# Attention scores of 16 heads in two row strips of the TensorE array instead of one padded stack

## What is computed

```python
scores = jnp.einsum('bhid,bhjd->bhij', Q, K) / math.sqrt(DH)
scores = scores + _alibi_bias(L, scores.dtype)[None]
attn = jax.nn.softmax(scores, axis=-1)
x = jnp.einsum('bhij,bhjd->bhid', attn, V)
...
y = jax.nn.silu(xf @ wg) * (xf @ wu) @ wd        # each expert, weighted by the router
```

## Time and profile before

| | us |
|---|---|
| median of 3 runs | 236.56 |
| lowest and highest | 236.47, 237.14 |
| the profiled execution | 235.97 |
| its span, first to last instruction | 234.2 |

### The profile page before, as it was taken

How to read it: one execution, slowest core, us unless ns; L and a number is a source line. 1 busy time by engine, 2 the same in 40 slices (tenths; PEclk the granted TensorE clock), 3 DMA queues, 4 the chain that set the end, 5 groups by cost and what they waited for, 6 DMA issues and landing times.

```text
span 234.2 us, 6086 instructions
## 1 busy us (share of the span) xinstructions
PE 213.8 (91%) x1942; PEld 175.4 (75%) x1942; DVE 175.9 (75%) x612; ACT 118.3 (51%) x283; POOL 74.4 (32%) x178
## 2 busy tenths in 40 slices
PE   2969787979999999999999999999999899989995
PEld 2757455757788787977897878878897779768884
DVE  4599636995699678985899569957985788653891
ACT  8565656466426734475346443663367234763310
POOL 2500016010860159013921094107700580038000
PEclk9999999999999999999999999999999999999999
DMA  5553586223312470317032612325123600250000
GB/s 157 175 90 105 125 215 205 80 69 99 87 48 60 83 172 3 104 52 199 3 102 49 157 44 60 84 78 131 38 70 88 165 0 4 84 126 0 1 25 22
DMA packets 13079, 20.24 MB, mean 86 GB/s; under 512 B 2800, under 2 KB 9440, under 8 KB 12544
## 3 DMA queue, kind: packets, MB, share of 16 engines
q1 hardware_dynamic: 12080, 18.64, 31.2%
q10 hardware_dynamic: 976, 1.32, 1.8%
HBM read 16.03 MB, written 3.78 MB: 85 GB/s over the span
## 4 chain that ended last, share of the span: by engine, by line
issue 33%; PE 31%; DVE 17%; POOL 11%; ACT 3%; DMA 1%; DVEq 1%; ACTq 0%; POOLq 0%; SPq 0%
POOL hid L1314 6%; DVE nmax L971 6%; PE ps_up L511 5%; PE ps_pv L444 4%; PE ps_m L537 4%; PE ps_st L425 3%; PE ps_pv L451 3%; PE ps_up L516 2%; DVE tg L1075 2%; DVE stacks_sb L1202 1%; PE ps_up L308 1%; DMA ident<-in_c_ident 1%; DVE hid L1081 1%; PE ps_m L466 1%; POOL ve L1278 1%
## 5 line engine op out<-in xcount | busy, mean ns | idle before, releaser
L791 ACT ACTIVATE th<-ps_up 128x256 f32<-128x256 f32 x72 | 27.6, 383 | 35.5 <-PE ps_up L516 34.8
L735 ACT ACTIVATE probs<-ps_st 128x512 f32<-128x512 f32 x64 | 37.0, 595 | 16.3 <-PE ps_st L425 11.1
L537 PE MATMUL ps_m<-wd_sb,hid 128*128 128x128 f32 x288 | 44.8, 283 | 0.0
L971 DVE TENSOR_REDUCE nmax<-ps_s 128x4 f32<-128x512 f32 x64 | 41.9, 680 | 0.4 <-issue 0.4
L1075 DVE SCALAR_TENSOR_TENSOR tg<-th,ps_up 128x256 f32<-128x256 f32 x72 | 29.8, 414 | 13.5 <-ACT th L791 13.2
L1314 POOL TENSOR_TENSOR hid<-hid,crep 128x256 f32<-128x256 f32 x56 | 39.1, 732 | 0.2 <-issue 0.2
L537 PEld LDWEIGHTS ps_m<-wd_sb,hid 128*128 128x128 f32 x288 | 37.6, 191 | 1.0
L1081 DVE TENSOR_TENSOR hid<-tg,ps_up 128x256 f32<-128x256 f32 x72 | 29.7, 413 | 1.0
L511 PE MATMUL ps_up<-x_hi,wg_hi 128*128 128x256 f32 x72 | 26.6, 369 | 0.4 <-ACT x_hi L772 0.2
L1278 POOL TENSOR_TENSOR ve<-mv,eps_sb 128x1 f32<-128x1 f32 x16 | 3.0, 191 | 69.5 <-DVE mv L1022 69.5
L425 PE MATMUL ps_st<-stacks_sb 98*128 98x128 f16 x256 | 24.8, 220 | 0.2
(11 more groups left out here) (147 smaller groups left out, 434.2 us busy)
## 6 DMA issues: line engine op xcount, KB each, us to landing
crep<-cw_dram SPq DMA_DIRECT2D x28, 256.0 KB, 4.6
stacks_sb<-qk_dram SPq DMA_DIRECT2D x32, 128.0 KB, 3.4
qk_dram<-qk_parts SPq DMA_DIRECT2D x16, 128.0 KB, 1.8
out_y<-x_all SPq DMA_DIRECT2D x8, 128.0 KB, 4.6
wg_sb<-in_wgT ACTq DMA_DIRECT2D x1, 576.0 KB, 3.5
wu_sb<-in_wuT ACTq DMA_DIRECT2D x1, 576.0 KB, 3.3
wd_sb<-in_wd SPq DMA_DIRECT2D x1, 576.0 KB, 4.1
x_all<-in_x SPq DMA_DIRECT2D x2, 256.0 KB, 4.2
```

What stands on the lines that cost most here:

```text
L537: last = mm(ps_dn[:, b * P:(b + 1) * P], hid[:, buf, c, b * P:(b + 1) * P], wd_sb[:, c, :], start=(c == 0 and b == 0), stop=(c == SHARED), ...
L735: fn(probs[:, b, g * HG * P:(g + 1) * HG * P], scores_bank(a, g)[:], ACT.Exp).then_inc(exp_sb, 1)
L791: fn(th[:, c % 2, :], ps_up[c % 2][:, 0, :], ACT.Tanh, scale=0.5).then_inc(tanh_sb, 1)
L971: v.tensor_reduce(nmax[:, b, HG * g:HG * g + HG], ps_s[g % 2][:].rearrange("p (h j) -> p h j", h=HG), AX_X, ALU.max, negate=True).then_inc ...
```

## The change

The 16 heads are cut into two strips of 8. Strip 0 keeps its rows at partitions 0 to 33 and strip 1 at 64 to 97 (32 rows of data and two for the shift), so there are no zero rows and no memsets for them, and a tile holds 8 heads instead of 16 per partition. The products have 32 rows (`scores`) or 34 (`scores_T`) and sit in a part of the array: tiles of 32x128 and of 64x128 at row 0 and at row 64. `scores` and `scores_T` now make two groups per call, with heads of strip 0 and strip 1 in turn into two banks, and wait until both banks have been read. `ORDER` maps the position of a group to its heads (0, 2, 1, 3). Each stack DMA becomes two of half the size, and so does each `shift_rows`; the k stacks of group p now wait for the shift rows of the sequence b = 0 of group p - 1, as the q stacks did for b = 1. The orders of PE, DVE and ACT are rewritten to suit.

```diff
+STRIP = 64
 SROWS = 4 * DH
-ZROWS = 96
-AROWS = ZROWS + 2
+AROWS = SROWS + 2
+HS = H // 2
+ORDER = (0, 2, 1, 3)
...
         qk_parts = sb("qk_parts", [P, 2, 2, T], F16)
-        stacks_sb = sb("stacks_sb", [AROWS, 2, 2, H, T], F16)
+        stacks_sb = sb("stacks_sb", [STRIP + AROWS, 2, 2, HS, T], F16)
...
-        nsplit = sb("nsplit", [P, NB, 2, H], F16)
+        nsplit = sb("nsplit", [P, NB, 2, 2, HS], F16)
...
                 sp.wait_ge(s_kd, 32 * p + 32)
+                if not at_start(p):
+
+                    sp.wait_ge(s_nm[0], 32 * p)
                 for plane, row in ((2, 0), (3, 2 * DH)):
-                    src = bass.AP(qk_dram.tensor, (buf * 5 + plane) * (P * T), [[H * T, 2 * DH], [1, H * T]])
-                    sp.dma_start(stacks_sb[row:row + 2 * DH, buf, 1].rearrange("r h t -> r (h t)"), src).then_inc(s_stack, 16)
...
+                    for s in range(2):
+                        src = bass.AP(qk_dram.tensor, ((buf * 5 + plane) * P + s * HS) * T, [[H * T, 2 * DH], [1, HS * T]])
+                        at = STRIP * s + row
+                        sp.dma_start(stacks_sb[at:at + 2 * DH, buf, 1].rearrange("r h t -> r (h t)"), src).then_inc(s_stack, 16)
...
-                    sp.wait_ge(s_nm[1], 16 * p)
+                    sp.wait_ge(s_nm[1], 32 * p)
                 for row in (0, 2 * DH):
-                    src = bass.AP(qk_dram.tensor, buf * 5 * (P * T), [[H * T, 2 * DH], [1, H * T]])
-                    sp.dma_start(stacks_sb[row:row + 2 * DH, buf, 0].rearrange("r h t -> r (h t)"), src).then_inc(s_stack, 16)
+                    for s in range(2):
+                        src = bass.AP(qk_dram.tensor, (buf * 5 * P + s * HS) * T, [[H * T, 2 * DH], [1, HS * T]])
+                        at = STRIP * s + row
+                        sp.dma_start(stacks_sb[at:at + 2 * DH, buf, 0].rearrange("r h t -> r (h t)"), src).then_inc(s_stack, 16)
...
-            def scores(a, b, g, buf):
-
-
-
-                bank, n = ps_s[g % 2], 2 * NHG * a + NHG * b + g
-                if b == 0 and g == 0:
-                    pe.wait_ge(s_stack, 64 * a + 64)
+            def scores(a, b, j, buf):
+
+
+                n = 2 * NHG * a + NHG * b + 2 * j
+                if b == 0 and j == 0:
...
                 else:
-                    pe.wait_ge(max_sb, n - 1)
-                if g == 0:
-                    mm(bank[:], dist16[:], slope_hi[:, 0:HG, :], start=True, stop=False, skip_group_check=True)
-                for h in range(HG * g, HG * g + HG):
-                    o = (h - HG * g) * P
-                    last = mm(bank[:, o:o + P], qs[buf][0:ZROWS, h, b * P:(b + 1) * P],
-                              ks[buf][0:ZROWS, h, b * P:(b + 1) * P],
-                              start=(g > 0), stop=True, skip_group_check=True)
-                last.then_inc(s_mm, 1)
+                    pe.wait_ge(max_sb, n)
+                if j == 0:
+                    mm(ps_s[0][:], dist16[:], slope_hi[:, 0:HG, :], start=True, stop=False, skip_group_check=True)
+                for k in range(HG):
+                    for s in range(2):
+                        row, h = STRIP * s, HG * j + k
+                        last = mm(ps_s[s][:, k * P:(k + 1) * P], qs[buf][row:row + SROWS, h, b * P:(b + 1) * P],
+                                  ks[buf][row:row + SROWS, h, b * P:(b + 1) * P], start=(j > 0 or s > 0), stop=True,
+                                  skip_group_check=True)
+                        if k == HG - 1:
+                            last.then_inc(s_mm, 1)
...
-            def scores_T(a, b, g, buf, f=None):
-
-                bank, n = scores_bank(a, g), 2 * NHG * a + NHG * b + g
-                seeded = not at_start(a) and (b, g) in ((0, 0), (1, 0), (1, 1))
+            def scores_T(a, b, j, buf, f=None):
+
+                n = 2 * NHG * a + NHG * b + 2 * j
+                seeded = not at_start(a) and (b, j) != (0, 1)
...
                 if seeded and b == 0:
                     pe.wait_ge(seed0_sb, a)
                 elif seeded:
-                    pe.wait_ge(seed1_sb, 2 * a + g - 1)
-                elif not (at_start(a) and b == 0 and g < 2):
-                    pe.wait_ge(exp_sb, n - 1)
-                if g == 0:
-                    pe.wait_ge(s_nm[b], 16 * a + 16)
...
+                if not (at_start(a) and b == 0 and j == 0):
+                    pe.wait_ge(exp_sb, n)
+                if j == 0:
+                    pe.wait_ge(s_nm[b], 32 * a + 32)
...
-                first = False if seeded else bias(bank, g)[0]
-                for h in range(HG * g, HG * g + HG):
-                    o = (h - HG * g) * P
-                    last = mm(bank[:, o:o + P], ks[buf][:, h, b * P:(b + 1) * P], qs[buf][:, h, b * P:(b + 1) * P],
-                              start=first, stop=True, skip_group_check=True)
-                    first = False
-                last.then_inc(st_mm, 1)
...
+                first = [False if seeded else bias(scores_bank(a, 2 * j), ORDER[2 * j])[0],
+                         bias(scores_bank(a, 2 * j + 1), ORDER[2 * j + 1])[0]]
+                for k in range(HG):
+                    for s in range(2):
+                        row, h = STRIP * s, HG * j + k
+                        last = mm(scores_bank(a, 2 * j + s)[:, k * P:(k + 1) * P], ks[buf][row:row + AROWS, h, b * P:(b + 1) * P],
+                                  qs[buf][row:row + AROWS, h, b * P:(b + 1) * P], start=first[s], stop=True,
+                                  skip_group_check=True)
+                        first[s] = False
+                        if k == HG - 1:
+                            last.then_inc(st_mm, 1)
...
                 scores(a, 0, 0, abuf)
-                scores(a, 0, 1, abuf)
                 if p is not None:
                     project_q(p)
                     project_k(p)
                 late_down(0)
-                scores(a, 0, 2, abuf)
                 late_down(1)
                 expert_in_T(f)
-                scores(a, 0, 3, abuf)
+                scores(a, 0, 1, abuf)
                 late_down(2)
                 up(f, 0)
+                up(f, 1)
                 scores(a, 1, 0, abuf)
-                up(f, 1)
-                scores(a, 1, 1, abuf)
                 shift_T(a, 0)
                 router(f)
                 late_down(3)
-                scores(a, 1, 2, abuf)
                 up(f, 2)
+                scores(a, 1, 1, abuf)
                 late_down(4)
-                scores(a, 1, 3, abuf)
                 up(f, 3)
                 late_down(5)
-                scores_T(a, 0, 0, abuf)
+                scores_T(a, 0, 0, abuf, f=f)
                 late_down(6)
-                scores_T(a, 0, 1, abuf, f=f)
                 shift_T(a, 1)
                 late_down(7)
                 second_half(f, a, p, q, abuf)
             def second_half(f, a, p, q, abuf):
                 up(f, 4)
-                scores_T(a, 0, 2, abuf)
+                scores_T(a, 0, 1, abuf)
                 weights_T(f, a)
-                scores_T(a, 0, 3, abuf)
                 up(f, 5)
-                if not at_start(f): down(f - 1, (8,), abuf)
                 scores_T(a, 1, 0, abuf)
                 weigh_values(a, 0, f)
+                if not at_start(f): down(f - 1, (8,), abuf)
                 scores_T(a, 1, 1, abuf)
-                scores_T(a, 1, 2, abuf)
                 values_T(a, 0)
                 up(f, 6)
-                scores_T(a, 1, 3, abuf)
                 attention_T(a, 0, f)
                 up(f, 7)
                 weigh_values(a, 1)
...
+                g = ORDER[i]
+                act.wait_ge(st_mm, 2 * NHG * a + NHG * b + i + 1)
+                if i == 0 and not at_start(a):
                     act.wait_ge(pv_mm, 2 * a + b - 1)
-                fn(probs[:, b, g * HG * P:(g + 1) * HG * P], scores_bank(a, g)[:], ACT.Exp).then_inc(exp_sb, 1)
+                fn(probs[:, b, g * HG * P:(g + 1) * HG * P], scores_bank(a, i)[:], ACT.Exp).then_inc(exp_sb, 1)
...
             def shift_rows(a, b, buf):
                 act.wait_ge(nm_sb, 2 * a + b + 1)
-                act.dma_start(qs[buf][ZROWS:AROWS, :, b * P:(b + 1) * P], nmT[:, b, :]).then_inc(s_nm[b], 16)
+                for s in range(2):
+                    act.dma_start(qs[buf][STRIP * s + SROWS:STRIP * s + AROWS, :, b * P:(b + 1) * P],
+                                  nmT[H * s:H * (s + 1), b, :]).then_inc(s_nm[b], 16)
...
             def seed(a, g):
-                dve.wait_ge(exp_sb, 2 * NHG * a + NHG + g - 1)
-                v.tensor_copy(ps_st[(g + 1) % 2][:], bias_T[:, g, :]).then_inc(seed1_sb, 1)
+                dve.wait_ge(exp_sb, 2 * NHG * a + NHG - 1 + 2 * g)
+                v.tensor_copy(ps_st[1][:], bias_T[:, g, :]).then_inc(seed1_sb, 1)
...
-            v.memset(stacks_sb[:, 0, 0].bitcast(F32), 0.0).then_inc(dve_pads, 1)
...
-            v.memset(stacks_sb[:, 1].bitcast(F32), 0.0).then_inc(dve_pads, 1)
```

105 lines of the change are left out of this document (44 added, 61 removed).

## The result

The changed kernel takes **262.70 us** (median of 4 runs, 259.69 to 264.15) where the kernel before takes 236.51 us (235.94 to 237.14): a ratio of **1.106, interval 1.097 to 1.116**. The forecast was 252.6 us in a range of 236 to 262. Direction and main mechanism were right; the loss is 26 us where 16 were forecast, and the median lies 0.7 us above the range (as a ratio, 1.106, it is just inside: 262 to 236.56 is 1.108). The profiled execution took 264.15 us, with a span of 262.3 us. The four runs differ more than those of the kernel before, and they go with the mean granted clock of TensorE: 0.974 in the one of 259.69 us, 0.941 and 0.948 in the others.

The account below looks back on a forecast made before the run. It took PE (91% busy) as nearly the bound, but its hand-over with ACT and DVE as deciding. 235.97 + 12.3 (seven steps) + 3.7 (first group) = 252.0 us profiled, 252.6 forecast; range 236 to 262.

Parts of the forecast that it names:

- main mechanism: Steps: PE waits on ACT and DVE; six lag 1.9 us each, the last 0.9, 12.3 us in all.
- the block with three biases: Second half of a step: PE waits 1.0 us for ACT's exponential and starts 1.76 late; 0.5 wait at the next block.
- The second DMA: Second half, ACT: two half-size shift DMAs cost between nothing and 0.62 us more to issue; taken at 0.5.
- the tiles: Score blocks: products in pairs gain 1.8 us per step; switches of 0.09 and exposed weight loads cost 1.4.
- The rival without overlap: Score blocks: paired products run one after the other, 1.8 us more per step, 260 us; no overlap or worse 0.05.
- the one that loses the fast load: Score blocks: products 0.11 us apart, a block 0.88 for 0.22, 5 us per step, 289 us; within that 0.05.
- TensorE's list: PE's own work in a step: 0.4 us shorter, bounds 1.8 shorter and 1.4 longer.
- what follows in the second half: From the block with three biases to `up` chunk 7: 6.1 us where it was 5.92; step lag 1.9.
- the first half: `x2_low` behind two `qk_low`, maxima 1.07 us later; second transpose of the maxima at 123.75 against 122.99.
- the first group at full clock: First group, no expert work between its blocks: 3.7 us longer, between 2 and 5.
- Faster: Whole kernel: waits for both banks are covered and PE stays the bound, 231 us; chance 0.16.
- Half of it: Steps: gaps close, only the 1.0 us wait at the block with three biases stays, 242 us; chance 0.13.

Follow-up runs that it names:

- twos alone: The changed kernel with its order in groups of two, but the stacks, DMAs and full-height products of before: 255.45 us, ratio 1.076.
- twos alone with it added: The twos alone with the DMA of the shift rows issued in two halves, one of each row: 261.78 us, ratio 1.107.
- the kernel with more fillers: The changed kernel with 36 more filler products where TensorE waits in the first group: 258.12 us, ratio 1.086.
- The step with the exponential first: The changed kernel with ScalarE's second exponential ahead of the copy and DMAs of the shift rows of b = 1: 260.58 us, ratio 1.098.
- the best arrangement tried: The twos alone with 36 more fillers, `x2_low` first and the exponential ahead of the shift rows: 246.37 us, ratio 1.036.
- the three kernels with `x2_low` put first: The changed kernel with `x2_low` ahead of both `qk_low`, 258.27 us; also with 36 fillers and exponential first, 247.66; all three edits on twos alone, 246.37.

## Why the prediction was right, and where it was too small

**Right, a step up to the block with three biases and the one behind it.** From a step's mask product to the block with three biases the forecast had 15.46 us (126.18 - 110.72), and the trace has 15.42 (200.60 - 185.18). TensorE waits 0.98 us there for 1.0 forecast. The next block starts 2.35 us later for 2.30, its wait is 0.43 for 0.5. The second DMA was taken at 0.5 us more and is 0.66; twos alone with it added shows what it is worth.

**Right, the tiles.** Strips overlap fully (0.056 us per pair), the switch costs 0.09 either way. The rival without overlap is out, and so is the one that loses the fast load. (Its 16 loads per block are double what the trace has, one for each of the eight products, which halves its 1.7 us; no term rests on it.) TensorE's list was put at 0.4 us less per step, and its busy time is 0.04 less: 0.14 less by the strips, 0.10 more by the order.

**Too small, what follows in the second half.** The steps f = 1 to 5 lag 2.2 us for 1.9, 1.5 us in all. It isn't the first half: there the second transpose of the maxima comes 0.58 us later than before (12.85 us after the mask product for 12.27), against 0.76 forecast. The delay was foreseen, though not that it stands as idle time, in waits of 0.30, 0.24 and 0.38. From this transpose to the block with three biases it is 2.57 us (200.60 less 198.03) where the forecast had 2.43, and from the block to `up` chunk 7 6.32 for 6.1. The 0.22 more arise late: from the first block of b = 1 (202.95) to the last (205.17, forecast 2.0 us on) TensorE's own work alone takes 2.22 us, with no wait listed, and the transposes of the values start 4.90 us after the block with three biases instead of 4.7:

```profile
205.17 0.40 PE L428 MATMUL ps_st<-stacks_sb 34*128 34x128 f16 x8
205.50 0.66 PE L456 MATMUL ps_pv<-ident,pv_sb 128*128 128x128 f32 x4
...
206.92 0.36 PE L516 MATMUL ps_up<-x_hi,wg_hi 128*128 128x256 f32 x1
```

**Too small, the first group at full clock.** 3.7 us forecast, 5.25 in the kernel with more fillers (41.64 for 36.39). There the first exponential is 2.7 us late (28.31 for 25.57) where 2.1 were put, and from it to the second `weigh_values` it takes 9.2 us (37.50 less 28.31) where 8.3 were put and the earlier trace rows have 6.7.

**Missing, the clock.** This is the step that failed. The forecast read off the page of before that the clock "is granted in full, 2.4 GHz, in every slice" and carried that over without a term for it, though it had itself put gaps into a first group in which nothing covers TensorE. The price is 4.8 us in the first group (46.48 less 41.64) and, by an estimate, most of the 3.9 that f = 0 takes beyond its 1.9: the twos alone ran f = 0 at a granted clock of 1.00 in 25.53 us, and with the 0.48 us by which a step of the changed kernel is longer it would be 26.0 and not 29.67. That is 3.7 us for 17.0 at half clock, a lower rate than in the first group. The sum, against the profiled execution's 12.15 us over the forecast of 252.0: first group 6.4 (4.8 clock, 1.6 size), f = 0 3.9, five steps 1.5, the rest of the span 0.4.

**The rivals.** "Faster" needed the exponential within 1.4 us of the transpose of the maxima; it ended 2.5 after (200.55 less 198.03). The step with the exponential first shows that this wait can be removed, and that TensorE's list is still not the bound. "Half of it", 242 us, is lower than the best arrangement tried, 246.4.

**What stays open.** Why the clock fell in later steps of two of the kernels and not of the changed one itself is argued from the waits of the first half (x2n, `x_lo`, maxima, transposes); in the profiles of the three kernels with `x2_low` put first it never fell behind f = 0. But neither did it in the two profiles of the changed kernel itself, and no run changed these waits one by one.

## What to carry to other kernels

A tile in a row strip pays only in a block that is long enough for its entry and exit: here a block of eight gained 0.22 us and paid 0.185 (0.05 more ahead of a float32 product), and the kernel lost more than the rest to one more DMA issue on the engine that everything waited for. Two buffers that are filled and waited for together are one buffer: the partner's hand-over falls out of cover, and costs 1.7 us per step with no tile in sight. And where a change makes TensorE wait in a stretch without other work for it, count that stretch's time at the lower clock as well, and look at the clock's row of the profile before any other.

## What the runs showed of the hardware

- The clock costs by itself: with 23 filler products less and every other instruction the same, the kernel before ran 10.4 us at 1.2 GHz and took 3.5 us longer. The price of one us at that clock was 0.36 us in two stretches, 0.44 in another and, by an estimate, 0.22 in a third. In one kernel, filling the first group only moved the fall to later steps.
- A DMA's issue on ScalarE takes 0.62 us whether it carries both shift rows of sixteen heads or half of that.
- Products of 32 or 34 rows in two strips start 2 to 4 ns apart, and a pair takes the time of one full-height product. Going into the strips costs 0.096 us and coming out 0.089, with the bias product or the down product as the neighbour; behind the exit the second float32 product is another 0.05 late.
